# A graph layer on one core: the stages ahead of the main loop reordered

## The reference

```python
h = relu(layernorm(x))                         # 6250 x 64
e = relu(concat([h[dst], edge_attr]) @ W1.T + b1)
e = relu(e @ W2.T + b2)                        # 206250 x 128
agg = segment_sum(e, src) / max(count(src), 1)
z = relu(concat([h, agg, u[0]]) @ Wa.T + ba)
out = x + z @ Wb.T + bb
```

## Time and profile before

| what | value |
|---|---|
| median of 3 runs | 1965.5 us (1960.17 to 1968.19) |
| profiled execution, its own time | 1965.07 us |
| its span | 1963.3 us |
| TensorE clock granted, mean | 0.954 of full |
| PE / DVE / ACT / POOL busy | 1728.9 / 1383.5 / 1116.8 / 1536.2 us |
| chain that ended last | POOL 46%, PE 21%, issue 16%, DMA 10%, DVE 6% |

### The profile page before, as it was taken

One profiled execution on the slowest core, in us unless ns is written; L12 is line 12 of the kernel. 1 busy time (PEld: TensorE's weight loads), 2 busy tenths in 40 slices (PEclk: granted clock), 3 DMA queues, 4 the chain that ended last, 5 costly groups with the idle time before them and its releaser, 6 DMA issues.

```text
span 1963.3 us, 42045 instructions
## 1 busy us (share of the span) xinstructions
PE 1728.9 (88%) x12463; PEld 1473.0 (75%) x12463; DVE 1383.5 (70%) x3570; ACT 1116.8 (57%) x2531; POOL 1536.2 (78%) x983
## 2 busy tenths in 40 slices
PE   3498888899999999999999999999999999977817
PEld 2376777688888787888878888887888888866715
DVE  7876566677677777777767777777777777744528
ACT  3275666566666665666656666666566666632203
POOL 6078888888888888888888888888888888887850
PEclk9699899999999999999999999999999999988959
DMA  7598888899999999999999999999999999997756
GB/s 268 198 197 154 140 154 150 170 193 199 182 197 205 195 196 197 192 205 188 193 195 194 191 204 192 197 198 206 199 188 203 198 200 204 202 213 148 155 125 197
DMA packets 321982, 372.08 MB, mean 190 GB/s; under 512 B 42432, under 2 KB 203552, under 8 KB 321248
## 3 DMA queue, kind: packets, MB, share of 16 engines
q1 hardware_dynamic: 185280, 306.11, 54.4%
q0 software_dynamic: 135360, 62.15, 33.7%
q10 hardware_dynamic: 1120, 1.11, 0.2%
HBM read 203.93 MB, written 159.27 MB: 185 GB/s over the span
## 4 chain that ended last, share of the span: by engine, by line
POOL 46%; PE 21%; issue 16%; DMA 10%; DVE 6%; ACT 1%; SPq 0%; POOLq 0%; ACTq 0%; DVEq 0%
POOL sums L797 40%; DMA sums<-regA,idx 8%; PE bank L1228 5%; POOL sums L785 5%; PE bank L1276 5%; PE bank L1250 4%; PE bank L1239 3%; PE bank L1266 2%; ACT regA L894 1%; DVE regC L1127 1%; DVE regC L986 1%; DVE regC L992 1%; DVE regC L1081 1%; DMA src<-rows_src 1%; DMA regC<-in_src_cols 1%
## 5 line engine op out<-in xcount | busy, mean ns | idle before, releaser
L797 POOL DMA_INDIRECT sums<-regA,idx x844 | 1354.7, 1605 | 324.0 <-issue 242.9
L1228 PEld LDWEIGHTS bank<-h,regC 128*128 128x128 f32 x3072 | 393.9, 196 | 209.7 <-ACT h L906 174.2
L1228 PE MATMUL bank<-h,regC 128*128 128x130 f32 x3072 | 427.9, 283 | 89.5 <-ACT h L906 89.1
L1276 PE MATMUL bank<-w,h 128*128 128x128 f32 x3224 | 435.3, 279 | 0.0
L1250 PE MATMUL bank<-regA,L 128*128 128x512 f32 x806 | 422.5, 606 | 2.9 <-DVE regA L1046 2.4
L1276 PEld LDWEIGHTS bank<-w,h 128*128 128x128 f32 x3224 | 402.5, 196 | 1.0 <-ACT h L886 0.6
L894 ACT ACTIVATE regA<-bank 128x520 f32<-128x520 f32 x211 | 127.3, 603 | 409.4 <-DMA sums<-regA,idx 351.1
L886 ACT ACTIVATE h<-bank 128x512 f32<-128x512 f32 x403 | 238.6, 592 | 156.1 <-PE bank L1250 144.2
L1239 PE MATMUL bank<-regC 128*128 128x129 f32 x2352 | 300.0, 281 | 15.7 <-ACT vscat L917 9.2
L1266 PEld LDWEIGHTS bank<-h,regC 128*128 128x128 f32 x1688 | 222.6, 192 | 118.2 <-issue 95.8
L906 ACT ACTIVATE h<-bank 128x512 f32<-128x512 f32 x403 | 239.8, 595 | 122.4 <-PE bank L1276 119.1
(11 more groups left out here) (142 smaller groups left out, 1279.3 us busy)
## 6 DMA issues: line engine op xcount, KB each, us to landing
regC<-slots SPq DMA_DIRECT2D x294, 260.0 KB, 5.0
regA<-in_ea SPq DMA_DIRECT2D x202, 256.0 KB
slots<-regC SPq DMA_DIRECT2D x192, 260.0 KB
src<-rows_src SPq DMA_DIRECT2D x107, 256.0 KB
slots<-regC SPq DMA_DIRECT2D x192, 138.1 KB
sums<-regA,idx POOLq DMA_INDIRECT x844
dstR<-rows_dst SPq DMA_DIRECT2D x101, 128.0 KB
sums<-zeros SPq DMA_DIRECT2D x20, 645.0 KB, 7.3
```

What stands on the lines that cost most here:

```text
L797: nc.gpsimd.indirect_dma_start(out=sums[k], out_offset=bass.IndirectOffsetOnAxis(ap=idx[:, n % RING, t:t + 1], axis=0), in_=scat[:, n % 4, ...
L1228: last = T.matmul(psSlot(t)[:, k, :], place, h2[:, g % 2, t, :], start=True, stop=True)
L1276: last = T.matmul(psL2(g % 2)[:, t * H:(t + 1) * H], h1[:, g % 2, t * TILE:(t + 1) * TILE], w2[:, :], start=False, stop=True, skip_group_c ...
```

## The change

- x is loaded and normalised in three pieces of 4, 4 and 5 chunks, their DVE steps interleaved; ACT runs one square root early on a dummy tile.
- b1 leaves p. It becomes the bias of the first relu of each group (L886). The copy of p from PSUM moves from DVE to ACT.
- 784 columns instead of 832 are counted (196 odd groups). POOL's single-operation `tensor_scalar` instructions become two-operation ones (with "times 1.0" or a fused step); `unitF` moves to DVE; three of the seven planes of the second digit, the 16-bit copy of `src` and `toscrap` move to POOL.
- The one-hot planes are laid out as (pack, digit, 16 tiles), so that 16 values of a plane lie side by side, and are made in two parts of 336 and 448 columns.
- Counting rounds hold up to eight packs over two banks (`ROUNDS`: 4+1, five times 4+4, 4). The sum over units is done on PE, accumulating in one bank with a shifted slice of `gpad`; one reduction and one comparison follow at the end, on DVE.
- `same` is now 112 x 448, made by seven selects on POOL behind `DERIVED`; POOL passes them before it starts on `srcF`.
- SP: four zeroings come ahead of the weights, five behind them, p is stored in three pieces with the rows stores between them; the other nine zeroings sit in steps 0 to 3. In a step the load of dst rows comes ahead of the window load.

```diff
-HALVES = [(0, 7), (7, NCH)]
+PIECES = [(0, 4), (4, 8), (8, NCH)]
-ZFIRST, ZMID = 9, 2
-ZAFTER = (0, 1, 1, 1, 1, 1, 2, 2)
+ZEARLY, ZFIRST, ZMID = 4, 9, 2
+ZAFTER = (1, 2, 3, 3)
-ODD = 208
+ODD = 196
+ROUNDS = [[(0, 4), (4, 5)]] + [[(a, a + 4), (a + 4, a + 8)] for a in range(5, 45, 8)] + [[(45, 49)]]
+DIGITS_AT = (0, PACK * ROUNDS[EARLY][0][0], NS)
+HOT_DVE = 4
-        A1 = take(NS * BA // 2).bitcast(bf16).rearrange("p (a c) -> p a c", c=BA)
+        A1 = take(NS * BA // 2).bitcast(bf16).rearrange("p (n c a) -> p n c a", c=BA, a=PACK)
...
+            for k in range(ZEARLY):
+                zero(k)
...
+            for k in range(ZEARLY, ZFIRST):
+                zero(k)
             store_p(0)
+            sp.wait_ge(dst8_ready, 1)
+            sp.dma_start(rows_dst, ...)
             store_p(1)
+            sp.wait_ge(src16_ready, 1)
+            sp.dma_start(rows_src..., src16[:, :, :])
             for k in range(ZMID):
                 zero(ZFIRST + k)
+            store_p(2)
...
+            for c in range(BA):
+                if c:
+                    pool.wait_ge(consts, CONSTS + 6 + c)
+                nc.gpsimd.affine_select(out=same[:, :, :, :], in_=same[:, :, :, :], compare_op=ALU.not_equal, fill=1.0, ...)
+            pool.wait_ge(consts, CONSTS + DERIVED + MASKED)
...
+            whole(G.tensor_scalar(quots, odd, 1.0 / NBIN, -(NBIN - 1) / (2.0 * NBIN), ALU.mult, ALU.add))
+            whole(G.tensor_scalar(quot, quot, MAGIC, 1.0, ALU.add, ALU.mult))
+            whole(G.tensor_scalar(quot, quot, MAGIC, -float(NBIN), ALU.subtract, ALU.mult))
...
-                nc.scalar.activation(h1[:, s % 2, :], psL1(s % 2), ACT.Relu).then_inc(h1_ready, 1)
+                nc.scalar.activation(h1[:, s % 2, :], psL1(s % 2), ACT.Relu, bias=b1c[:, :]).then_inc(h1_ready, 1)
...
+            for c in range(BA):
+                one_hot(A2, quot, c, 0)
+            for c in range(HOT_DVE):
+                one_hot(A1, unitF, c, 0)
...
+            for c in range(BA):
+                one_hot(A2, quot, c, 1)
+            spill_over(0)
+            for c in range(HOT_DVE):
+                one_hot(A1, unitF, c, 1)
+            for k in range(1, len(ROUNDS)):
+                spill_over(k)
+            dve.wait_ge(spill_used, len(ROUNDS))
...
+            for k in range(len(ROUNDS)):
+                count_tiles(k)
+                if k >= 1:
+                    add_totals(k - 1)
+            add_totals(len(ROUNDS) - 1)
```

More of the change, by code:

```diff
@@ L677, in whole @@
                 pool.wait_ge(bin_step, bstep[0])
[L679 to L682, removed]
             pool.wait_ge(src_cols_in, 16)
-            G.iota(srcF[:, NT:NTP], [[0, NTP - NT]], base=0, channel_multiplier=1, allow_small_or_imprecise_dtypes=True).then_inc(srcF_ready, 1)
@@ L700, in _ @@
+            pool.wait_ge(unitF_ready, 1)
+            for n in range(2):
+                a0, a1 = DIGITS_AT[n], DIGITS_AT[n + 1]
+                for c in range(HOT_DVE, BA):
+                    G.tensor_scalar(A1[:, a0 // PACK:a1 // PACK, c, :], unitF[:, a0:a1].rearrange("p (n a) -> p n a", a=PACK), float(c), 1.0, ALU.is_equal, ALU.mult).then_inc(hot_ready[n], 1)
+            G.tensor_scalar(toscrap[:, :], srcF[:, :], -1.0, scrapc[:, :], ALU.mult, ALU.add).then_inc(toscrap_ready, 1)
             pool.wait_ge(mode_ready, 1)
-            pool.wait_ge(table_stored, 32)
+            pool.wait_ge(table_stored, 16 * len(PIECES))
@@ new lines, in _ @@
+            square(0)
+            root(0)
+            square(1)
+            evac_hT(0)
+            for c in range(1, NCH + 1):
+                if c < NCH:
+                    evac_hT(c)
+                evac_p(c - 1)
+                if c == 1:
+                    root(1)
+                if c == 2:
+                    square(2)
+                if c == 3:
+                    root(2)
+                if c == 5:
+                    act.wait_ge(dstR_ready, 1)
+                    nc.scalar.activation(dst8[:, :, :], dstR[:, :, :], ACT.Copy).then_inc(dst8_ready, 1)
@@ L989, in _ @@
             dve.wait_ge(consts, CONSTS + DERIVED)
[L990 removed]
+            dve.wait_ge(digits_ready, 1)
+            dve.wait_ge(binF_ready, 1)
+            VE.scalar_tensor_tensor(out=unitF[:, :], in0=quot, scalar=-float(BA), in1=binF[:, :], op0=ALU.mult, op1=ALU.add).then_inc(unitF_ready, 1)
             for c in range(BA):
[L992 to L993 removed]
@@ L994, in _ @@
-            for k in range(NPACK // 4):
-                dve.wait_ge(spill_psum, k + 1)
-                wait(dve, spilt_ready, k - 1)
-                VE.scalar_tensor_tensor(out=spill[0:wide, k % 2, :, :], in0=bank[0:wide, 4 + k % 2, 0:4 * wide].rearrange("p (a c) -> p a c", c=wide), scalar=float(CAP),
-                                       in1=same[:, :, :].rearrange("p a c -> p (a c)").unsqueeze(1).broadcast_to([wide, 4, wide]), op0=ALU.max, op1=ALU.mult).then_inc(spill_ready, 1)
-                dve.wait_ge(spill_ready, k + 1)
-                with nc.allow_low_precision("whole numbers up to 156"):
-                    VE.tensor_reduce(spilt[:, 4 * k:4 * k + 4], spill[0:wide, k % 2, :, :], axis=AX.X, op=ALU.add).then_inc(spilt_ready, 1)
+                one_hot(A2, quot, c, 0)
@@ new lines, in _ @@
+            dve.wait_ge(unitF_ready, 1)
+            for c in range(HOT_DVE):
+                one_hot(A1, unitF, c, 0)
+            dve.wait_ge(consts, CONSTS + DERIVED + MASKED)
+            with nc.allow_low_precision("zeros and ones"):
+                VE.tensor_reduce(group4, same[:, 0, 0, :].rearrange("p (g t) -> p g t", t=TPG), axis=AX.X, op=ALU.add).then_inc(group4_ready, 1)
+            for c in range(BA):
[3 more added lines that the diff above has]
+                one_hot(A1, unitF, c, 1)
@@ L1149, in _ @@
             pe.wait_ge(consts, CONSTS + DERIVED)
-            pe.wait_ge(w1_in, 48)
+            pe.wait_ge(zeroed, 4)
+            for k in range(2):
+                last = T.matmul(psL2(k), ident[:, :], zeros[:, 0:GE], start=True, stop=True)
+            last.then_inc(seedable, 1)
+            pe.wait_ge(w1_in, 32)
             for c in range(NCH + 1):
                 if c < NCH:
-                    for n, (c0, _) in enumerate(HALVES):
+                    for n, (c0, _) in enumerate(PIECES):
                         if c == c0:
```

322 lines of the change are left out of this document (173 added, 149 removed).

## The result

The changed kernel takes 1948.77 us (median of 5, 1942.78 to 1952.38) against 1965.5 before (five runs by now, the same median): ratio 0.9908, interval [0.9888, 0.9929]. That is 16.7 us faster, in the direction forecast, but 20 us short of the 37 us forecast, and outside the range (1918 to 1944). The profiled execution took 1948.77, span 1947.0.

What follows compares the result with a forecast made beforehand. POOL's scatter stream bounds the kernel, so only the fourth scatter's start counts: 33.1 us from the loop's start plus 5.1 from the zeroing wait less 1.5 gives 36.7 off 1965.07, so 1928 us; range 1918 to 1944.

Steps and rivals of the forecast that it cites:

- What bounds the kernel: POOL's scatters and the gaps of about 0.3 us between them fill nearly the whole loop; compute is held back.
- T: Start of POOL's fourth scatter: forecast at 71.2 us against 107.9 before, 36.7 sooner.
- The chain ahead of the loop: Masks, digits, planes, counting rounds and mode: the loop's first one-hot at 52.6 us instead of 85.70, 33.1 sooner.
- Digits: POOL's digit instructions ahead of the loop: ready at 27 us, with 3 us allowed for blocking by DVE.
- Rounds and `mode`: Counting rounds taken at 8.4 us, then reduction, comparison, matmuls and threshold 1.9; mode at 52.3 us.
- p, SP's queue and the floor: Transfers started ahead of the loop need 46 us, landing about 3; first window in by 51, nearly touching 52.6.
- Zeroings: Nine zeroings in SP's queue among the early windows, 5.9 MB or 16 us: 1.5 us later for the fourth scatter.
- The rival on the transfers: SP's steps and the last zeroing set the fourth scatter: T 75 to 77, time about 1933; chance 0.15.
- The 11.0 from the loop's start to the first scatter: From the loop's first one-hot to POOL's first scatter: 11.0 us, kept as in the kernel before.
- the stream of 937 takes 1789 us whatever the other engines do: From the fourth scatter to the end of the last, POOL's time stays 1789 us.
- Bias in the relu: ACT's first relu of each group 687 ns against 592, 38 us in all, hidden under 351 us of waiting.
- The rival of a denser meeting of POOL and DVE: In the loop, stretched scatters double: 51 us more, time 1979, mean scatter 1.65 us; chance 0.03.

Runs made afterwards that it cites:

- planes_dve: The changed kernel with all planes made on DVE, none on POOL; 1944.67 us, ratio 0.9883.
- zero_step4: The changed kernel with three late zeroings in steps 0 and 1 and the last six behind step 4's loads; 1939.60 us, ratio 0.9845.
- zero_gap3: The changed kernel with three late zeroings issued while SP waits for the table and six behind step 4's loads; 1938.83 us, ratio 0.9859.
- the two pairs: The changed kernel and zero_gap3, each against itself with the old load order from step 4 on; streams 1797.4 against 1790.3, 1794.4 against 1792.4 us.
- single_op: The changed kernel with three of POOL's fused two-operation digit instructions put back to a single operation; one run, 1954.65 us, not used.

## Why the prediction was right and wrong

**What bounds the kernel: right.** POOL's scatters follow at 0.3 us in every kernel, and the time follows the fourth scatter: over eleven kernels T ranges over 35 us and what is behind it over 8.

**The chain ahead of the loop: right as a sum, 52.61 for 52.6,** by terms that cancel, and in part by luck, since kernels with the same work there gave 52.5 to 53.6. Masks 7.2 (8.2 taken). Digits ready at 30.3, not 27. Six two-operation instructions took 13.5 us on POOL where 0.84 each would be 5.0: blocking by DVE cost 8.5, and 3 was allowed (bounds 0 and 6). L703 alone took 3.9 of it, beside DVE's `dstR` and last scaling. The row's 3.98 for the two-input instruction held such a wait already: it took 2.02 (3.7 taken), and this and the masks gave part back.

From the digits to the end of the planes and the first clipping the sum had 15.0 us, of which 3 for POOL's work; it took 12.2. Of the 3 came 2.6. `unitF` took 2.58, not 0.9, and ended 0.8 us behind POOL's cast (30.21 + 1.89); seven planes of 448 took DVE 3.15 us beside POOL's planes and 2.19 in planes_dve, without them. The planes themselves would have been 8.1 without that, 10 taken. The prediction had priced POOL's plane parts at 0.43 each from an instruction of 0.88 that writes side by side; they took 1.84 in the mean, with three of 336 columns at 1.34, and no run has one without DVE beside it, so how much of this is blocking is not shown. Rounds and `mode` took 10.0 for 10.3, although a sum on PE took 0.57 in the mean (L1267) and not 0.4.

The mutual blocking that the Trainium skill states (Advanced Engine Details and Errata, Mode Summary), there of VectorE instructions that use the second port, is in the trace in both directions. DVE's pass of 1024 elements (L1002) took 2.54 when it started beside POOL's cast of 12.59 to 14.12, and 1.23 beside its masks.

**p, SP's queue and the floor: right in order.** The third store of p was issued at 37.3, it landed at 48.4 (46 and a landing were reckoned), and the window load came at 49.44. The floor touched the chain: PE's first matmul of the loop came 1.6 us behind the one-hot (54.16 and 52.61), where before it was 0.8 (86.49 and 85.70).

**The failed step is "Zeroings".** It said that they stand "in SP's queue between the windows of steps 1 to 4", that "steps 2 to 4 come 1 to 4 us late" and "I take 1.5 on T". T came 12.8 later than the sum that held this 1.5, and with the same bytes placed elsewhere it was 8.0 (zero_step4) and 11.0 us sooner (zero_gap3). I priced the windows for PE, and did not follow who else is queued behind a late load: the destination rows of step 4 gate DVE's step 3, and behind them in DVE's order are the indices of group 0. The load was 10.5 us in landing, and DVE waited 6.65 for it behind 5.83 for a matmul that was late itself. The rival on the transfers had the place and the right sign, with 75 to 77 for T; 84 came.

**The 11.0 from the loop's start to the first scatter was taken over unchanged, and was too small.** In zero_gap3 it is 14.2, and this is what is left of the error in T. PE's first matmul came 2.7 us behind the one-hot, waiting for its window. It then ran at a granted clock of 0.50 of full, the lower of its two levels, until about 61; before, the clock was 1.00 from 90 us on, 3.5 us behind PE's first matmul. In the changed kernel, where PE stood waiting for late loads, it was down again from 62 to 68 and from 76 to 80.

**The second failed step is "the stream of 937 takes 1789 us whatever the other engines do".** It took 1797.4, and 7.8 of the 8.3 us are longer scatters. The new order of loads within SP's steps, which stands in the change's description, had no term at all in the sum. It is worth 5 to 6 us by the column "behind", and 7.1 and 2.0 by the streams of the two pairs. SP's queue was followed ahead of the loop and not within its steps.

**Bias in the relu: right**, at 90 ns a time, hidden. The rival of a denser meeting of POOL and DVE was set to show as a mean scatter above 1650 ns; it is 1610. It did happen at a sixth of the size priced: 7.8 us of longer scatters against 51.

**The range** ended at 1944 on the slow side because each rival was priced alone; the transfer rival and a slower stream happened together. The transfer rival was also priced too low: with its 1933 and the 8.3 us of the stream the time would still have been inside.

What stays open is how late source rows lengthen the stream of scatters. Late loads come and go with the order, and with them, less sharply, the stream. The added time is in the scatters (1610 against 1605 ns, and 1592 against 1556 for those of the overflow), not in waits; that DVE's shifted work meets them more often is a guess that no run tests. Nor was the price of each reordered part ahead of the loop (three pieces, larger rounds, sums on TensorE) measured by itself; only their sum.

## What to carry to other kernels

Before a queue's work is packed into fewer steps, ask how far the queue runs ahead of the compute: the same four numbers of `ZAFTER` cost nothing with 28 us of lead and 11 us on T with 3. Follow a late load through the engine that waits for it in order, down to the first instruction behind it that the bound needs. And put a wait in a queue behind the issues that do not need it: one load moved ahead of another in the loop went with some 5 us more behind T, of the 23.9 that the whole new beginning won ahead of it.

## What was not expected of the hardware

- Moving 5.9 MB of zeroings from SP's queue to ACT's freed the small loads on SP's only in part: the first scatter came at 73.50, against 78.05 with all of them among the loads and 67.36 with most behind them.
- The blocking of POOL and DVE cost both. POOL's L703 took 4.75 us beside DVE's passes and 2.18 in a slower form without them; DVE's planes of 448 took 0.45 in the mean beside POOL's planes and 0.31 without.
- A POOL tensor_scalar with a single operation took 2.18 us for 784 columns (single_op) and 0.84 with a second, idle operation ("times 1.0").
